# Two attention layers in one stream of slots, with scores per head and values stored directly

## What is computed

```python
# third layer
q = (x @ Wq.T).reshape(B, N, 12, 32); k = (x @ Wk.T)...; v = (x @ Wv.T + bv)...
a = einsum('bnhd,bmhd->bhnm', q, k) * 384 ** -0.5 + adj[:, None]
a = where(all(a == 0, -1), -inf, a); a = nan_to_num(softmax(a, -1))
layer = einsum('bhnm,bmhd->bnhd', a, v).reshape(B, N, 384) @ Wo.T + bo
# fourth layer
q, k, v = split_heads(x @ Wq + bq), split_heads(x @ Wk + bk), split_heads(x @ Wv + bv)
s = einsum('bhqd,bhkd->bhqk', q, k) / sqrt(32) + beta * adj[:, None]
s = where(adj[:, None] > 0, s, -9e15)
layer = einsum('bhqk,bhkd->bhqd', softmax(s, -1), v) # heads joined again
```

## Time and profile before

| | us |
|---|---|
| median of 3 runs | 3090.41 (3089.36 to 3090.95) |
| profiled execution, device time | 3087.28 |
| its span in the trace | 3085.2 |
| PE busy (95% of the span) | 2926.5 |
| DVE busy (75%) | 2301.9 |
| POOL busy (45%) | 1375.3 |
| ACT busy (37%) | 1155.7 |

### The profile page before, as it was taken

The page is one execution under the profiler, slowest core; times in us unless marked ns, Lnnn a source line. Parts: engine busy times, 40 slices in busy tenths (PEclk is TensorE's granted clock), DMA queues, the critical chain, the costliest instruction groups (busy, mean ns, idle before and its releaser), DMA issues. The chain is left out here.

```text
span 3085.2 us, 57599 instructions
## 1 busy us (share of the span) xinstructions
PE 2926.5 (95%) x22080; PEld 2491.0 (81%) x22080; DVE 2301.9 (75%) x5311; ACT 1155.7 (37%) x2369; POOL 1375.3 (45%) x1207
## 2 busy tenths in 40 slices
PE   8999999999599999999999599999999789999997
PEld 7988888889488888888887488888888677888886
DVE  6788888888557766766775688888888667777777
ACT  3344443444322222222222234434443234444443
POOL 6755576556465555555554232222222212332233
PEclk9999999999799999999999799999999999999998
DMA  5121121111211101100110111101111011111111
GB/s 141 31 68 47 50 62 58 61 47 54 87 54 49 39 25 35 49 29 25 45 49 11 55 51 45 45 23 45 45 33 36 34 37 45 46 45 46 56 45 44
DMA packets 134641, 145.98 MB, mean 47 GB/s; under 512 B 56800, under 2 KB 132320, under 8 KB 134368
## 3 DMA queue, kind: packets, MB, share of 16 engines
q1 hardware_dynamic: 134368, 142.31, 14.9%
HBM read 91.96 MB, written 50.33 MB: 46 GB/s over the span
## 5 line engine op out<-in xcount | busy, mean ns | idle before, releaser
L1908 POOL TENSOR_TENSOR l_prob<-l_prob,l_mx 128x512 f32<-128x512 f32 x192 | 200.7, 1045 | 774.9 <-DVE l_mx L1745 774.9
L1135 DVE TENSOR_TENSOR l_val<-l_ring,l_vec 64x384 f32<-64x384 f32 x512 | 284.6, 556 | 75.6 <-PE l_ring L950 68.7
L950 PE MATMUL l_ring<-whi,l_hhi 128*128 128x384 f32 x1152 | 272.8, 345 | 5.8 <-POOL wlo L79 5.8
L950 PE MATMUL l_ring<-wlo,l_hhi 128*128 128x384 f32 x1152 | 263.4, 336 | 0.0
L950 PE MATMUL l_ring<-whi,l_hlo 128*128 128x384 f32 x1152 | 263.3, 336 | 0.0
L1499 PE MATMUL l_ring<-l_hhi,whi 128*128 128x512 f32 x576 | 234.9, 408 | 9.5 <-DVE l_hlo L1725 9.2
L680 POOL TENSOR_TENSOR l_hlo<-l_hf,l_hhi 128x512 fp32r<-128x512 f32 x96 | 128.5, 1362 | 256.0 <-DVE l_hhi L477 256.0
L1499 PE MATMUL l_ring<-l_hlo,whi 128*128 128x512 f32 x576 | 228.8, 397 | 0.0
L1499 PE MATMUL l_ring<-l_hhi,wlo 128*128 128x512 f32 x576 | 228.8, 397 | 0.0
L445 ACT ACTIVATE l_mt<-l_ring 128x512 f32<-128x512 f32 x192 | 115.2, 600 | 292.0 <-PE l_ring L345 292.0
L950 PEld LDWEIGHTS l_ring<-whi,l_hhi 128*128 128x128 f32 x1152 | 200.7, 189 | 24.6 <-issue 18.6
(11 more groups left out here) (211 smaller groups left out, 7050.2 us busy)
## 6 DMA issues: line engine op xcount, KB each, us to landing
l_hf<-xt SPq DMA_DIRECT2D x16, 864.0 KB, 5.5
l_x<-x SPq DMA_DIRECT2D x16, 768.0 KB, 4.5
x<-l_za SPq DMA_DIRECT2D x16, 768.0 KB, 4.5
x<-l_zb SPq DMA_DIRECT2D x16, 768.0 KB, 3.6
l_xa<-x SPq DMA_DIRECT2D x16, 768.0 KB, 4.9
l_xb<-x SPq DMA_DIRECT2D x16, 768.0 KB, 6.5
x<-l_zfa SPq DMA_DIRECT2D x8, 768.0 KB, 3.5
x<-l_zfb SPq DMA_DIRECT2D x8, 768.0 KB, 4.3
```

The costliest lines, as they stand in the source:

```text
L950: mm = nc.tensor.matmul(ring[k % RING][:, 0:D], hh[:, c, first:first + P], ww[:, c, :], start=(j == 0), stop=(j == len(terms) - 1))
L1135: ins = nc.vector.tensor_tensor(val[half, (g + b) % GRAPHS, 0:D], ring[k % RING][half, 0:D], bias[half, :], ALU.add)
L1908: nc.gpsimd.tensor_tensor(row, row, mx[:, c, ts, :].rearrange("p t h -> p (t h)").unsqueeze(2) .broadcast_to([P, 2 * HP, S]), ALU.subtract)\
```

## The change

`heads_pass` is called once, for 32 slots: n = 0 to 15 are the groups of layer 3, n = 16 to 31 those of layer 4, in one block, unrolled. `project(n)` says which layer a slot belongs to. Names now have the prefix `h_`.

- Keys are stored unpadded, like the queries, and ACT evacuates both in one instruction each. Their clearing is gone. Scores are made per head: stationary 32 rows by 64 queries, moving 64 key columns, 32 matmuls a chunk in place of 8. They go head by head; each set of four for one PSUM bank waits on `head_done` until the set of the head before is finished in that bank.
- The order is chunk by chunk. `query_key(n, 0..5)` makes query 0, key 0, query 1, key 1, ..., in slot n itself, and the scores of a chunk follow directly behind its key product. PE waits there for ACT's evacuation. Values come behind all scores; the outputs of the last tile move into the next slot, between its first two products.
- `values_out` writes all values to their place, four DVE instructions a tile, two of them with input and output on different partitions. `vside`, `swap`, the side multiplications and ACT's copies are gone.
- `output` alternates the two graphs for each pair instead of doing one graph after the other.
- `final_apply` moves from DVE to ACT (128 by 384, four in a slot). POOL's addition of the bias in layer 3 is four instructions instead of one.
- The input transposes go to the score banks and `ring[1]` at the end of a slot.

```diff
             def chunk_scores(n, c):
+                pe.wait_ge(qk_evac, 2 * KC * n + 2 * c + 2)
                 pe.wait_ge(s_evac, UNITS * n + 2 * c)
-                for g in range(GRAPHS):
-                    p0, t = S * (g % 2), g // 2
-                    mm = nc.tensor.matmul(scores[t // 2][p0:p0 + S, (t % 2) * HP * S:(t % 2 + 1) * HP * S],
-                                          q[:, c, g * S:(g + 1) * S], keys[:, c, g, :, :].rearrange("p h j -> p (h j)"),
-                                          start=True, stop=True)
+                for h in range(HP):
+                    head = slice(HD * h, HD * h + HD)
+                    for u in range(2):
+                        if h:
+                            pe.wait_ge(head_done, (KC * n + c) * 2 * (HP - 1) + 2 * (h - 1) + u + 1)
+                        for t in (2 * u, 2 * u + 1):
+                            for b in range(2):
+                                graph = slice((2 * t + b) * S, (2 * t + b + 1) * S)
+                                first = (t % 2 * HP + h) * S
+                                mm = nc.tensor.matmul(scores[u][S * b:S * b + S, first:first + S], q[head, c, graph],
+                                                      keys[head, c, graph], start=True, stop=True)
+                        if h < HP - 1:
+                            mm.then_inc(head_done, 1)
...
-                for b in range(2):
-                    rows = slice(S * b, S * b + S)
-                    for m in range(PAIRS):
+                for m in range(PAIRS):
+                    for b in range(2):
+                        rows = slice(S * b, S * b + S)
                         mm = nc.tensor.matmul(ot[t % 2][rows, 2 * m * HO:2 * (m + 1) * HO], probt[t % 2][:, m, rows],
...
+                query_key(n, 0)
+                if n:
+                    output(n - 1, 3)
+                query_key(n, 1)
+                chunk_scores(n, 0)
+                query_key(n, 2)
+                if before:
+                    outputs_turned(n - 1, range(0, 2))
+                query_key(n, 3)
+                if before:
+                    outputs_turned(n - 1, range(2, 4))
+                chunk_scores(n, 1)
+                query_key(n, 4)
+                query_key(n, 5)
+                chunk_scores(n, 2)
                 pe.wait_ge(qk_evac, 2 * KC * (n + 1))
...
+                if before:
...
+                    result(n - 1, 0)
+                    result(n - 1, 1)
+                    pe.wait_ge(w_evac, T * (n - 1) + 1)
+                    value(n, 0)
+                    pe.wait_ge(w_evac, T * (n - 1) + 2)
+                    result(n - 1, 2)
...
+                else:
+                    value(n, 0)
+                    value(n, 1)
+                    probs_turned(n, 0)
+                    pe.wait_ge(v_evac, T * n + 1)
+                    value(n, 2)
+                    probs_turned(n, 1)
+                    output(n, 0)
+                    pe.wait_ge(v_evac, T * n + 2)
+                    value(n, 3)
+                probs_turned(n, 2)
+                output(n, 1)
+                if n + 1 < slots:
+                    rows_turned(n + 1)
+                probs_turned(n, 3)
+                output(n, 2)
+            output(slots - 1, 3)
...
+            def values_out(n, t):
...
+                for b in range(2):
+                    rows = slice(S * b, S * b + S)
+                    for p in range(2):
+                        ins = nc.vector.tensor_tensor(val[S * p:S * p + S, 2 * t + b, :, p, 0:HD], src[rows, :, p, :],
+                                                      bias[rows, :, p, :], ALU.add)
+                ins.then_inc(v_evac, 1)
```

More of the change, by code:

```diff
@@ L1474, in rows_transposed, with query_key @@
                                                  sh.ident[:, :])
                     mm.then_inc(t_done, 1)
-            def products(out, terms):
+            def query_key(n, k):
+                w, m = weight(n, k % 2), k // 2
+                if k >= 2:
+                    pe.wait_ge(qk_evac, 2 * KC * n + k - 1)
+                elif k == 1:
+                    pe.wait_ge(lo_done, KC * (n + 1))
+                else:
+                    pe.wait_ge(v_evac, max(T * n - 1, 0))
+                for c in range(KC):
+                    if k == 0:
+                        pe.wait_ge(lo_done, KC * n + c + 1)
+                    for j, (ww, hh) in enumerate(((sh.whi[w], hhi), (sh.whi[w], hlo), (sh.wlo[w], hhi))):
+                        mm = nc.tensor.matmul(ring[k % 2][:, :], ww[:, c, m * P:(m + 1) * P], hh[:, c, :],
+                                              start=(c == 0 and j == 0), stop=(c == KC - 1 and j == 2))
+                mm.then_inc(qk_done, 1)
@@ L1519, in sides, with value @@
-            def sides(n, ts):
-                for t in ts:
-                    if project and t == 0:
-                        pe.wait_ge(olo_done, T * n)
-                    pe.wait_ge(v_evac, T * n + t + 1)
-                    if t >= 2:
-                        pe.wait_ge(side_evac, T * n + t - 1)
-                    nc.tensor.matmul(pt[t % 2][:, 0:PAIRS * HD], sh.swap[:, :],
-                                     vside[:, t % 2, :, :].rearrange("p m f -> p (m f)"),
-                                     start=True, stop=True).then_inc(side_done, 1)
+            def value(n, t):
+                b = t % 2 if not project(n - 1) else (0, 0, 0, 1)[t]
+                rows = slice(t * P, (t + 1) * P)
+                row_major(lambda c: hhi[:, c, rows], lambda c: hlo[:, c, rows], weight(n, 2), ring[b][:, 0:D])\
+                    .then_inc(v_done, 1)
@@ L1623, in _, with result @@
-            slots(pe, body)
-            if project:
-                pe.wait_ge(w_evac, T * (groups - 1))
-                outputs_transposed(groups - 1, range(T))
-                results(groups - 1, range(T), True)
+            def result(n, t):
+                pe.wait_ge(olo_done, T * n + t + 1)
+                row_major(lambda c: ohi[:, t, c, :], lambda c: olo[:, t, c, :], weight(n, 3), ring[0 if t == 0 else 1][:, 0:D])\
+                    .then_inc(w_done, 1)
+            pe.wait_ge(sh.w_ready, 15)
@@ L1963, in shared @@
     sh.const_in = sem("const_in")
-    sh.const_count = 16 * 5
+    sh.const_count = 16 * 4
     with nc.Block() as block:
```

729 lines of the change are left out of this document (322 added, 407 removed).

## The result

The changed kernel takes 3099.5 us (median of 9 runs, 3096.58 to 3101.36); the kernel before took 3090.2 us beside it. The ratio is 1.0032, 95% interval 1.0022 to 1.0042: 0.3% slower, where 1.7% faster was forecast. The profiled run has a span of 3099.0 us, against 3085.2 of before.

What follows compares the result with a forecast made beforehand. PE's own list was taken to set the pace. Terms of -13.3, -2.2, -51.1, +12.0 and +2.5 us gave together -52: 3033 us against the profiled span, 3038 against the median; range 2990 to 3095.

Steps and rivals of the forecast that it cites:

- Waits for the evacuation, new: PE waits for ACT after key products, 0.9 or 1.0 us each: 2.0 us a slot in layer 3, 3.0 in layer 4.
- No drop of the clock at the seam: Sign expected in the profile: the granted clock, 0.84 in the seam between the passes before, no longer drops there.
- Scores per head: Score chunks on PE, 64 records: 2.2 us a chunk against 1.97 before, +0.7 us a slot.
- The first rival: In the scores, PE's wait for itself does not overlap: 4.1 us a chunk, 3220 us in all; chance 0.10.
- the fourth: Small scores run together on different array rows: 1.9 us a chunk, DVE's alternation 0.3 us a slot less, 2999 us; chance 0.15.
- Weight loads: Weight loads bound the 64 column score matmuls: 3.3 us a chunk, 3144 us in all; chance 0.03.
- Outputs: Output multiplications alternating two graphs: 0.78 us a tile instead of 1.36, a gain of 2.3 us a slot.
- Behind the last scores: PE's delays after a slot's last scores, with less product work as cover: +0.7 us a slot in layer 3, +0.8 in layer 4.
- the DVE rival: DVE's bank alternation is longer, 0.8 us more in both kinds of slot: 3063 us, only the seam won; chance 0.20.
- Start and seam: Up to the first scores, -13.3 us; slots 1 to 15 of layer 3, which hold the seam, -51.1 us.
- Slot 0 and slot 1: Layer 3's first slots: slot 0 at 37.4 us against 39.6, slot 1 at 44.0 like the other slots to 15.
- The sum of the steady slots: All slot terms together: 44.0 us a slot in layer 3 against 44.75, 37.1 in layer 4 against 36.74.

Runs made afterwards that it cites:

- the run with 128 rows: Changed kernel with all 128 rows of queries and keys in each score multiplication instead of one head's 32 (sums over four heads): 3042.4 us, ratio 0.9852.
- reordered twice: Changed kernel, scores one product later, sums and values earlier, and layer 4's mask at the slot's start, statistics behind chunk 0's maxima: 2993.8 us, ratio 0.9691 to before.
- the three reorderings: Changed kernel with scores one product later (3039.1 us); then sums and values moved earlier too (3035.6); then DVE's mask and statistics moved in layer 4 too (2993.8).

## Why the prediction was wrong, step by step

The forecast's places, beside the changed kernel, the run with 128 rows and the last run (us, from the profiled executions):

| place | forecast | changed | 128 rows | reordered twice |
|---|---|---|---|---|
| up to the first scores of slot 0 | 1730.2 | 1730.7 | 1730.0 | 1732.0 |
| slot 0 | 37.4 | 40.0 | 40.0 | 39.2 |
| slots 1 to 15 of layer 3 | 660 | 689.8 | 661.9 | 644.0 |
| first slot of layer 4 | 43.7 | 46.9 | 43.9 | 42.2 |
| the 14 after it | 519.4 | 547.1 | 522.0 | 496.0 |
| to the end | 42.4 | 44.5 | 43.1 | 40.0 |
| sum | 3033 | 3099.0 | 3040.8 | 2993.5 |

- **The step that failed** is in "Waits for the evacuation, new", and in the sum above it: each wait was priced with its own 0.9 or 1.0 us and every duration was taken from stretches at a granted clock of 1.00. The change puts those waits directly ahead of 2.2 us of 32-row multiplications, and there the clock fell once or twice a slot. The changed kernel's span is 66 us above the forecast sum, and the run with 128 rows gives back 58 of these. The rows spoke of a clock at 0.84 and 0.80 only in the seam and the tail, and I read it as a thing of long drains. "No drop of the clock at the seam" was foretold, and the slot at the seam stands at 0.93, like its neighbours; that the clock would drop in every slot was no term, no rival and no part of the range. The range ended at 3095 and missed by 4.5 us.
- **Scores per head**: 2.2 us a chunk forecast, 2.16 measured. The 32-row shape costs the same as 128 rows in its own time. The first rival (no overlap, 4.1 us) is out, and so is the fourth (the small scores run together, 1.9 us); a wait for itself costs 0.03 us on the mean here (measured with 128 rows), with the other bank's set in between. The working by the chain of one bank came to the right sum, though the waits are nearly hidden in it and the multiplications' own pace of 31.4 ns makes 2.0 of the 2.16.
- **Weight loads**, the second rival: out, since the loads of the 6144 records of the scores keep up with a chunk of 2.0 to 2.2 us.
- **Outputs**: 0.78 us a tile forecast. A tile delays the next work by 0.85 us with the change of form. The gain was forecast as 2.3 us a slot; the group's busy time fell by 1.8 (174.2 to 117.9 us over 32 slots). The term was 0.5 us a slot too good.
- **Waits for the evacuation** by themselves: 2.0 and 3.0 us a slot; measured idle time is 0.69 twice and 0.78 three times, plus the 0.17 to 0.2 us to the modelled end: right within 0.3 us a slot.
- **Behind the last scores**, 0.7 and 0.8 us, and the DVE rival: too dark by some 0.6 us a slot. TensorE's waits for DVE's sums are 0.4 us in all of layer 3 and for values 2.0 us in both layers. DVE went from 83% to about 65% busy and bounds nothing in this order. Writing across partitions costs 355 ns, as the 353 that I took.
- **Start and seam**: right to 0.5 us at the first scores, and the seam is gone as described.
- **Slot 0 and slot 1**: too low, slot 0 by 2.6 us and slot 1 by 4.7 (44.0 forecast, 48.7 with 128 rows, 50.6 in the changed kernel). I had not seen that weights are still split in them: POOL's 5.7 us for the low parts hold up its subtraction, ACT's exponential and the key behind it (a wait of 3.4 us in slot 1), and the clock falls there too.
- **The sum of the steady slots**: 44.0 and 37.1 forecast, 43.8 and 37.3 with 128 rows. Their sum was right to 0.2 us, in part by luck: outputs 0.5 us too good and the waits behind the last scores 0.6 us too dark cancel. What fails in the changed kernel is that every term was taken at the full clock.

What stays open: whether the clock would also fall if the 32-row scores followed a wait of other length than 0.7 to 0.8 us, since that pair was not varied; what it is about fewer rows that matters; and why a fall comes in one chunk and not in the next of the same form.

## What to carry to other kernels

A price taken from a stretch at the full clock holds only if the new order keeps the clock up. Where a change puts an idle time next to multiplications that use a small part of the array's rows, forecast with a second case in which every slot has a stretch at the lower level, and look at the granted clock first when the result is in. And when a wait is moved, read what the waited-for engine has ahead of the work: the first two of the three reorderings here moved waits on more than away in layer 4, and only the third, which used DVE's idle stretch at the start of the slot, took most of them off.

## What the runs showed of the hardware that was not expected

- Idle time was not all that went with the granted clock: with the same waits and columns, scores of 32, 64 and 128 rows had it at 0.94, 0.99 and 1.00 in layer 4, and took 3099, 3056 and 3042 us.
- With 128 rows three waits of 1.5 us a slot left it at 1.00; with one wait of 2.66 us a slot it fell in some slots, with 128 rows and with 32 alike (0.98).
- A chunk of 64 multiplication records of 64 columns took 2.16 us with 32 rows and 2.18 with 128. Without TensorE's waits for its own earlier sets, with another set in between, it took 2.01 us with 128 rows, 31 ns a record; the six waits cost 0.17 us.
